# A four-layer recurrent block: attention of layers 0+1 and of layers 2+3 each as one row of 64 groups, the int4 gate network in slots of that row, the low-rank one behind the last scores

## The reference

```python
for l in range(4):                      # x: (4, 256, 512) float32
    xn = layernorm(x)                   # no learned weights
    s = attention[l](xn)                # 32 heads of 16
    g = silu(ffn[l](xn))
    x = x + s * g
# attention 0, 2, 3: rope, 8 key/value heads, causal mask; attention 1: 32 key/value heads, no mask, no rope
# ffn 0: octonion product with ternary weights (gate, up, down; hidden 1360)
# ffn 1: one 512x512 matrix, int4 with group zeros and scales, dequantised to float16, plus a bias
# ffn 2: silu(x W1') * (x W3') W2', 1792 hidden, weights with a scale per 128x128 block
# ffn 3: H = (x U1) V1 + b1 (rank 128, hidden 1376), (silu(H1) * H2) U2 V2 + b2
```

## Time and profile before

| | us |
|---|---|
| median of 3 runs | 1388.28 (1384.67 to 1388.38) |
| the profiled execution | 1391.96, its span 1390.2 |
| PE busy | 1238.0 (89% of the span) |
| DVE, ACT, POOL busy | 801.0, 648.6, 374.0 |
| chain that ended last, by engine | PE 74%, DVE 12%, ACT 9%, issue 4%, DMA 1% |
| mean granted TensorE clock | 0.945 |

### The profile page before, as it was taken

How to read it: one execution, slowest core, us unless ns; L and a number is a source line. 1 busy time by engine, 2 the same in 40 slices (tenths; PEclk the granted TensorE clock), 3 DMA queues, 4 the chain that set the end, 5 groups by cost and what they waited for, 6 DMA issues and landing times.

```text
span 1390.2 us, 22431 instructions
## 1 busy us (share of the span) xinstructions
PE 1238.0 (89%) x8844; PEld 920.6 (66%) x8844; DVE 801.0 (58%) x1309; ACT 648.6 (47%) x1100; POOL 374.0 (27%) x462
## 2 busy tenths in 40 slices
PE   4999889987696999987999999988998779889987
PEld 3888767764454565653678888876776557776764
DVE  8733556667504555475365555556666645566664
...
GB/s 273 1 1 0 1 1 3 1 3 100 31 0 1 1 2 2 2 2 95 99 91 91 91 91 93 66 0 3 2 2 3 132 31 1 1 2 3 2 3 62
DMA packets 11753, 48.33 MB, mean 35 GB/s; under 512 B 2809, under 2 KB 3838, under 8 KB 10370
## 3 DMA queue, kind: packets, MB, share of 16 engines
...
...
## 4 chain that ended last, share of the span: by engine, by line
PE 74%; DVE 12%; ACT 9%; issue 4%; DMA 1%; POOL 0%; SPq 0%; ACTq 0%; DVEq 0%
PE bank L518 19%; PE bank L670 14%; PE bank L548 9%; PE bank L802 7%; PE bank L766 6%; PE bank L715 4%; PE bank L684 3%; PE bank L747 3%; DVE negmaxs L1371 2%; ACT probsw L1049 2%; PE bank L776 2%; PE bank L612 1%; ACT pvs L1056 1%; ACT probss L1049 1%; PE bank L696 1%
## 5 line engine op out<-in xcount | busy, mean ns | idle before, releaser
L1568 POOL TENSOR_SCALAR_AFFINE_SELECT probss<-probss 128x512 f32<-128x512 f32 x192 | 125.4, 661 | 326.0 <-ACT probss L1049 325.1
L1371 DVE TENSOR_REDUCE negmaxs<-bank 128x4 f32<-128x512 f32 x192 | 174.2, 951 | 60.5 <-PE bank L724 60.2
L1049 ACT ACTIVATE probss<-bank 128x1024 f32<-128x1024 f32 x192 | 153.4, 813 | 63.6 <-PE bank L747 58.7
L1518 POOL TENSOR_TENSOR W_lo<-W_lo_whole,W_hi 128x1536 fp32r<-128x1536 f32 x28 | 98.1, 3505 | 135.8 <-ACT W_hi L903 135.8
L715 PE MATMUL bank<-kTs,qTs 64*128 64x128 f32 (+1 forms) x768 | 87.2, 320 | 19.2 <-DVE negmaxTs L1389 7.1
L903 ACT ACTIVATE W_hi<-W_lo_whole 128x1536 fp32r<-128x1536 f32 x28 | 41.7, 1488 | 132.8 <-DVE W_lo_whole L1257 132.8
L670 PE MATMUL bank<-Wqkv,xT_whole 128*128 128x512 f32 (+1 forms) x256 | 91.3, 513 | 7.3 <-DVE negmaxw L1371 4.0
L715 PEld LDWEIGHTS bank<-kTs,qTs 64*128 64x128 f32 x768 | 66.9, 202 | 42.8 <-issue 26.7
L1278 DVE TENSOR_TENSOR h_lo<-h_lo_whole,h_hi 128x512 fp32r<-128x512 f32 x50 | 73.3, 1466 | 34.9 <-ACT h_hi L925 34.9
L1371 DVE TENSOR_REDUCE negmaxw<-bank 128x4 f32<-128x1024 f32 x64 | 75.1, 1219 | 30.3 <-PE bank L715 29.6
L766 PE MATMUL bank<-probss,Vs 128*32 128x256 f32 (+1 forms) x1536 | 83.7, 336 | 7.8 <-DVE negmaxs L1371 4.7
...
## 6 DMA issues: line engine op xcount, KB each, us to landing
...
```

What stands on the lines that cost most here:

```text
L1049: nc.scalar.activation(A[l].probs[gi % 2][:, kb, :, q0:SEQ].rearrange("p (b h) q -> p b h q", b=2), B.tensor(key)[:, :, 0:2 * nq].rearrang ...
L1371: v.tensor_reduce(A[l].negmax[u % 2][:, qb, :].rearrange("p (b h) -> p b h", b=2)[:, :, 2 * g:2 * g + 2], B.tensor(key)[:, :, 0:2 * nk].re ...
L1518: gp.tensor_tensor(lo, whole, hi.bitcast(F32), ALU.subtract).then_inc(w_low.sem, 1)
L1568: gp.affine_select(out=blk, in_=blk, compare_op=ALU.is_ge, fill=0.0, base=0, pattern=[[0, 4], [1, P]], channel_multiplier=-1).then_inc(cau ...
```

## The change

**One row for two layers.** `RUN = 16` units: layers 0 and 1 are units U = 0 to 15 of run r = 0, layers 2 and 3 those of r = 1. A single loop goes over 64 slots. `unit(r, U)` and `group(r, G)` say whose unit or group it is, and all look-ahead (U+1, U+2, U+3, G+5) crosses from one layer to the next. The opening (`first_rows`) is done for layers 0 and 2 only. A layer's sequence b is normalised for the next layer while its other sequences are still in work: statistics at g = 3 of U = 3, 5, 7, 9, `scale_rows` at g = 0 of U = 4, 6, 8, 10, and one tile is transposed at g = 1 and g = 3 of these.

**ffn 1 in slots** of units 10 to 15: `unpack` in (10, 1), `group_values` with `dequantise` in (11, 1), (11, 3), (12, 0), (12, 1), and `tile1` in eight slots from (13, 0) to (15, 1), each with a silu on ACT. Layer 1's attention output waits in `gate[t]` (`store_rows`) for tiles 0 to 5 and is multiplied and added by `gate_rows`.

**ffn 2** takes into its first chunks what is left of attention 1 (last `weigh_values`, `turn_context`, `turn_rows`, `project_out`) and tiles 4 to 7 of its own transposes.

**ffn 3** stands behind the last slot. Only the multiplication by U1 (`low_rank_in`) is in slots (13, 1) and (13, 3); its weights are split in slots too (U = 2, 8, 10, 13, 14), all low parts on POOL. All 22 chunks, with LAG 2 in place of 3, come after the last scores, with the end of attention 3 in the first three; the bias b2 becomes two more matmuls per tile; `gate_rows` updates x, and the result is stored.

```diff
-LATE_TILES = (TILES - 2, TILES - 1)
-LAG = {0: 3, 2: 1, 3: 3}
+LAG = {0: 3, 2: 1, 3: 2}
+RUN = 2 * UNITS
+GROUP_SLOTS = {(11, 1): 0, (11, 3): 1, (12, 0): 2, (12, 1): 3}
+TILE1_SLOTS = {(13, 0): 0, (13, 1): 1, (13, 3): 2, (14, 1): 3, ...}
+LATE1 = 6
+LOW3_SLOTS = {(13, 1): 0, (13, 3): 1}
+SPLIT3_SLOTS = {(8, 0): 0, (8, 1): 1, (8, 2): 2, (13, 2): 3, (13, 3): 4, (14, 0): 5}
+def unit(r, U):
+    return 2 * r + U // UNITS, U % UNITS
...
+            def slot(r, G):                                   # TensorE
+                U, g = divmod(G, GROUPS)
+                l, u = unit(r, U)
+                scores_cols(l, u, g, 0)
+                if G + LEAD < RUN * GROUPS:
+                    scores_rows(r, G + LEAD, 0)
+                    scores_rows(r, G + LEAD, 1)
+                scores_cols(l, u, g, 1)
...
+                if g % 2 == 1 and U + 3 < RUN:
+                    project(*unit(r, U + 3), g // 2, QKV_BANK)
+                    filled_out = True
+                if r == 0 and (U, g) in TILE1_SLOTS:
+                    tile1(TILE1_SLOTS[U, g])
+                    filled_out = True
+                if r == 1 and (U, g) in LOW3_SLOTS:
+                    low_rank_in(LOW3_SLOTS[U, g])
+                    filled_out = True
...
+            def ffn2():
+                last = RUN * GROUPS - 1
+                for e in range(2 * HC2):
+                    gate_up(2, e, 2 * (e % 2))
+                    if e == 0:
+                        weigh_values(0, last, last)
+                        turn_context(0, last - 1, last)
+                        transposes(2, (4, 5), banks=(2, 3))
+                    if e == 1:
+                        turn_context(0, last, last)
+                        for tau in range(2):
+                            turn_rows(1, SEQS - 1, tau, 6 + tau)
+                    if e == 2:
+                        for tau in range(2):
+                            project_out(1, SEQS - 1, tau, 6 + tau)
+                        down(2, 0)
...
-            for l in range(LAYERS):
-                ffn(l)
-                attention(l)
+            ffn0()
+            first_rows(0)
+            for G in range(RUN * GROUPS):
+                slot(0, G)
+            ffn2()
+            first_rows(2)
+            for G in range(RUN * GROUPS):
+                slot(1, G)
+            ffn3()
...
+            def gate_rows(l, t):                              # VectorE
+                dve.wait_ge(*B.emptied(("O", l, t // 2, t % 2)))
+                dve.wait_ge(*B.emptied(("out", l, t)))
+                v.tensor_tensor(gate[:, t, :], gate[:, t, :], (silu1 if l == 1 else silu3)[t % 2][:],
+                                ALU.mult).then_inc(gated.sem, 1)
+                dve.wait_ge(*gated.at(l, t + 1))
+                v.tensor_tensor(x[:, t, :], x[:, t, :], gate[:, t, :], ALU.add).then_inc(x_done.sem, 1)
```

More of the change, by code:

```diff
@@ new lines, in program, with hidden_places @@
+        after_first = 101056
+        A = [attention_set(0, first, 0), attention_set(1, first, 0), attention_set(2, second, P), attention_set(3, second, P)]
+        def hidden_places(l, at_silu, at_h):
+            hid = [place(f"silu{l}_{i}", [P, 512], F32, at_silu) for i in range(2)], [], [], []
+            for i, start in enumerate(at_h):
+                at = [start]
+                hid[1].append(place(f"h{l}_hi{i}", [P, 512], F32R, at))
+                whole, lo = place_both(f"h{l}_lo{i}", [P, 512], at)
+                hid[2].append(whole)
+                hid[3].append(lo)
+            return hid
@@ L438, in program @@
         x_done = mark("x_updated", [TILES] * 4)
-        last_out = {l: ("out", l, TILES - 1) for l in range(LAYERS)}
         def chunk_used(l, e):
@@ L1668, in _ @@
[L1668 to L1678 removed]
+            sp.wait_ge(*B.filled(("ST", 1, UNITS - 2, GROUPS - 1, 1)))
```

1355 lines of the change are left out of this document (775 added, 580 removed).

## The result

| | us |
|---|---|
| before, in the same comparison | 1388.33 (1384.67 to 1392.09, 4 runs) |
| after | 1371.45 (1361.77 to 1376.63, 4 runs) |
| ratio after to before | 0.986, 95% interval 0.983 to 0.990 |
| the profiled execution | 1376.63, its span 1374.9 |

The account below looks back on a forecast made before the run. TensorE binds, losing time at the layer seams by idling and lower clock. Stages 183.6 + 434 + 2.5 + 288.7 + 347 + 81 give a 1336.8 us span, 53 less, so a 1335 us median; range 1307 to 1368.

Parts of the forecast that it names:

- five tile slots put at 6 to 7.7 us: First row, (13,1), (14,1), (14,2), (15,0), (15,1): each lasts as long as ScalarE with its silu and table loads, 6 to 7.7 us.
- The prediction's own sign of being wrong: It called itself wrong if the clock falls in a row, ffn 3's chunks take well over 2.1 us, or tile slots keep TensorE's pace.
- ffn 3 and the end: Last stage, behind the last slot: chunks, V2 tiles, end of attention 3, stalls and a serial end, together 81 us.
- Stalls in ffn 2 are 2 to 20, taken 6.: ffn 2 with layer 2's opening: TensorE's waits could only be bounded, 2 to 20 us, and 6 was put in the sum.
- `unpack`, some 20 small operations in one slot, 2.: First row, VectorE: unpacking in a single slot adds 2 us.
- U = 2 with 1.5 for weight splits: Row of layers 2 and 3: weight splits add 1.5 us to unit 2, and 1.5 to unit 8 likewise.
- 6 + 6 us put down for VectorE: Both rows: VectorE's added work costs 6 us each; the first row's holds 3 for scale_rows, 2 for unpack, 1 for statistics and dequantising.
- cross-check: Whole kernel: TensorE's busy 1238 less some 35 us of lower clock in removed openings, plus 4, gives 1207, 90% of 1337.
- number 2: Slots and ffn 3: other engines bind, added loads 17 us, scale_rows 6 and waits of 10 show fully: 1370 us; chance 0.20.
- Rival 1: Slots take the new work for nothing, as TensorE binds wherever it has work: 1312 us; chance 0.13.
- rival 3: First row, U = 10 to 15: TensorE loses its full clock, at 0.73 costing 61 us, so slower: 1396 us; chance 0.03.
- Rival 4: Order as said but the seam just moves, ffn 2 and ffn 3 each losing 25 us more: within 0.3%; chance 0.02.

Follow-up runs that it names:

- e9: The changed kernel itself, unedited, timed again beside a later batch of kernels: 1369.99 us, ratio 0.985 to the kernel before.
- e11: Changed kernel with the edits of e1, e2, e3, e5, e7, e8 and layer 1's last context ahead of ffn 2's second chunk: 1333.35 us, ratio 0.959.
- e1: Changed kernel with POOL's inverse_deviation(2, 3) in ffn 2 put behind the low part of weight chunk 3: 1361.51 us, ratio 0.981.
- e8: Changed kernel with VectorE's int4 unpacking spread over slots (10,1), (10,2), (10,3) and (11,0) instead of all in (10,1): 1365.97 us, ratio 0.982.
- e2: Changed kernel with weight splits for layer 3 and ffn 3 moved to slots g = 1 and g = 2, without rotation: 1362.67 us, ratio 0.980.
- e5: Changed kernel with the product with the values ahead of the out projection in slots g = 0 of odd units: 1361.52 us, ratio 0.979.
- e3: Changed kernel with VectorE's normalising of two tiles split between slots g = 0 and g = 2: 1363.77 us, ratio 0.982.
- e7: Changed kernel with layer 1's eight ffn tiles done two to a slot: 1367.71 us, ratio 0.984.
- e12: e11 plus, in each row's opening, unit 2's second projection ahead of the eight groups of scores: 1326.04 us, ratio 0.953.

## Why the prediction was wrong

The direction was right, and so was the main count: which work goes where and what a slot costs with it. Middle units came as forecast: U = 5 to 7 of the first row 31.2, 27.5 and 31.0 (30.9, 27.1, 31.7), U = 0 to 2 of the second 20.7, 18.4, 20.4 (20.7, 18.4, 20.8). Of the five tile slots put at 6 to 7.7 us, three are there at full clock ((13,1) 6.8 and (15,0) 6.7 after, (15,1) 7.6 in e9), while (14,1) is 5.7 after and (14,2) 8.9 in e9. The prediction's own sign of being wrong, a clock that falls in a row, is there: 0.90, 0.95, 0.86 and 0.87 in units 10, 13, 14 and 15 of the first, 0.88 to 0.94 in units 3, 5, 8 and 11 of the second.

For ffn 3 and the end, 78.6 us at full clock against 81 looks like a hit, and that is luck. It had 59 busy and 22 idle; e11 has 68.7 busy and 9.9 idle. V2 in twenty matmuls takes 6.2 us and not 4.6, and its second half (6.3 more) was not counted as busy; two chunks take 4.32, not 4.22; but the waits ahead of the serial end, put at 8, are 2.4, for neither LAG 2 nor the gating shows one. The terms as listed also add up to 83.5, unless the store is part of the 8.1.

What failed are four terms.

1. **"Stalls in ffn 2 are 2 to 20, taken 6."** The step listed the wait of `turn_rows` (3.3, it is 2.56) and chunk 4 (1 to 2, it is 3.7 before `down` and 2.9 before a later `gate_up`). It missed chunk 3: POOL's queue was not read. The change moved layer 1's last out projection into ffn 2, so that the variances for `inverse_deviation(2, 3)` come late, but left that operation ahead of the low part of chunk 3. Idle time of the stage went from 8.9 us before to 22.45. e1: 8 us in the stage.
2. **"`unpack`, some 20 small operations in one slot, 2."** e8 measures 6.1.
3. **"U = 2 with 1.5 for weight splits", "U = 8 with 1.5", and the waits in crowded slots.** The forecast counted 1.5 us in each of the two units. They cost more by what they hold up: VectorE's addition, then two row maxima, then a bank, then the out projection. e2 gives 4.6 and e5 4.7 (the same wait of the out projection, without POOL's part). Of the 6 + 6 us put down for VectorE, 2.3 come out when the normalising is split (e3). U = 15 of the second row, put at 8 us, takes 11.1 at full clock and 12.7 in the profile after.
4. **The clock.** The sum put no lower clock into the rows beyond that of their first unit, and its cross-check took some 36 us out with the openings. In the profile after, the mean clock is 0.953 (before 0.945), in the seven-edit kernel 0.975; worked out from these means, TensorE was at the lower level for about 153 us before, 129 after and 67 in e11. So the lower clock left the seams and came back in the rows. For the second row the seven profiles of one instruction stream price it: 8.3 us between 0.95 and 0.98. In the first row units 13 and 14 took 33.6 and 37.7 us against 30.2 and 33.4 forecast, and 31.9 and 33.6 where they ran at full clock. In ffn 3 and the end it is 84.4 at 0.88 against 78.6 at 0.99. Part of the lower clock stands behind the waits of points 1 to 3 and goes with them (3.8 of e1's 8.0, 2.75 of e8's 6.1); part differs between executions of the same instructions.

Of the rivals, number 2 (other engines bind in the slots and at ffn 3) had the amount, 1370 (its parts, 17, 6 and 10, make 33 and not 35). Its mechanism is right in kind and off in its list, so that the amount is in part luck: leaving the silus out was worth 12.3 us in units 13 and 14, 6.6 of them at full clock, where it had 17 for all loads; the second half of `scale_rows` 2.3, not 6; ffn 3 showed no added wait of size. It did name VectorE beside POOL's weight splits in the second row, which e2 bears out. The unpacking, POOL's order and the bank of the out projection were not in it. Rival 1 is refuted for this kernel, and so is rival 3: from U = 10 to 15 the clock was 0.86 to 1.00 after, not 0.73, and the kernel is faster. Rival 4 likewise, by the ratio's interval of 0.983 to 0.990.

That removing the waits takes 36.6 us off (1369.99 to 1333.35, against a forecast of 1335) shows that these waits, with the clock behind them, amount to what was missing. It doesn't show that each term of the sum was right: e11 lies 2.7 us over the forecast in the first row and 3.2 under it in ffn 2; two of its seven edits (those of e3 and e7) take out costs that the forecast had counted; and by the profiles 4.2 us of the difference between e9 and e11 lie in ffn 3, where no edit stands.

**What stays open.** Why the same row runs with the full clock in one execution and falls to half of it several times in another. Of ffn 3 with the end, the three profiles with paired tiles (e7, e11, e12) have 78.6 to 78.7 us and the ten others 81.8 to 84.4; whether that is chance isn't known, as each kernel has one profile. The waits ahead of the out projection were there in e7's row as well (1.79 us in slot (3,0), where the changed kernel's profile has 1.80, and 2.05 in (11,0)), and unit 3 ran at full clock behind it; so such a wait is not enough by itself for the clock to fall. No run here separates this further. Nor was it tried to load weight chunks 4 and 5 of ffn 2 earlier, where about 3.6 and 3 us of idle time remain in e11 and e12 too.
